# The second layer norm's output, made by VectorE in one pass

## The reference

```python
x = x + _L0_xattn_ref(_layernorm(x), ctx_1024, mask, Wq, bq, Wk, bk, Wv, bv, Wo, bo)
x = x + _L0_ffn_ref(_layernorm(x), theta, phi, theta_noise, phi_noise)

def _layernorm(x, axis=-1, eps=1e-05):
    m = jnp.mean(x, axis=axis, keepdims=True)
    v = jnp.var(x, axis=axis, keepdims=True)
    return (x - m) / jnp.sqrt(v + eps)

# in _L0_ffn_ref
real = jnp.einsum('bti,io->bto', x, jnp.cos(theta + theta_noise))
imag = jnp.einsum('bti,io->bto', x, jnp.sin(phi + phi_noise))
return jnp.sqrt(real * real + imag * imag)
```

## Time and profile before

| | us |
|---|---|
| median of 3 runs | 265.4 (264.9 to 266.73) |
| the profiled execution's own time | 265.45 |
| its span, first to last instruction | 263.6 |
| TensorE busy in the span | 238.0 (90%) |
| VectorE busy | 183.5 (70%) |
| ScalarE busy | 148.7 (56%) |
| GpSimd busy | 65.3 (25%) |

### The profile page before, as it was taken

How to read it: one execution, slowest core, us unless ns; L and a number is a source line. 1 busy time by engine, 2 the same in 40 slices (tenths; PEclk the granted TensorE clock), 3 DMA queues, 4 the chain that set the end, 5 groups by cost and what they waited for, 6 DMA issues and landing times.

```text
span 263.6 us, 3879 instructions
## 1 busy us (share of the span) xinstructions
PE 238.0 (90%) x1223; PEld 135.8 (52%) x1223; DVE 183.5 (70%) x348; ACT 148.7 (56%) x203; POOL 65.3 (25%) x158
## 2 busy tenths in 40 slices
PE   0989859868968799999999999999999999999991
PEld 0979523624633345644664476448545844444440
DVE  2037799996796779678787877787778663964442
ACT  0148667664713792678367647844593559266441
POOL 1000555572524403310331133023302310132000
PEclk9999967999979999999999999999999999999997
DMA  6999930269120797287539635783687244324531
GB/s 201 383 421 413 418 150 0 51 191 236 30 61 18 123 240 298 44 236 180 225 73 245 219 139 122 203 273 106 165 168 316 42 81 80 162 40 80 199 119 44
DMA packets 47948, 44.79 MB, mean 170 GB/s; under 512 B 42454, under 2 KB 42454, under 8 KB 44605
## 3 DMA queue, kind: packets, MB, share of 16 engines
q1 hardware_dynamic: 47269, 44.42, 55.7%
q10 hardware_dynamic: 664, 0.18, 0.4%
HBM read 25.66 MB, written 8.39 MB: 129 GB/s over the span
## 4 chain that ended last, share of the span: by engine, by line
PE 66%; DVE 16%; DMA 5%; POOL 5%; issue 4%; ACT 3%; SPq 1%; DVEq 0%; POOLq 0%; ACTq 0%
PE re L472 7%; PE re L474 7%; PE re L473 7%; PE im L472 7%; PE im L474 7%; PE im L473 7%; PE score_bank L427 6%; DVE angle_w L745 2%; PE att L461 2%; PE att L459 2%; DMA wk<-in_Wk 2%; DVE angle_w L748 2%; DMA xTb<-in_xT 2%; DVE stats L766 2%; DVE x L824 2%
## 5 line engine op out<-in xcount | busy, mean ns | idle before, releaser
L622 ACT ACTIVATE h<-x,shift,rstd 128x512 f32<-128x512 f32 x32 | 25.9, 810 | 40.7 <-POOL shift L348 40.7
L472 PE MATMUL re<-w_hi,hT 128*128 128x512 f16 x108 | 41.6, 385 | 4.2 <-DMA hT<-h_split 4.2
L472 PE MATMUL im<-w_hi,hT 128*128 128x512 f16 x108 | 40.9, 379 | 0.8 <-DVE w_lo L757 0.8
L474 PE MATMUL re<-w_hi,hT 128*128 128x512 f16 x108 | 41.4, 384 | 0.0
L473 PE MATMUL re<-w_lo,hT 128*128 128x512 f16 x108 | 41.4, 384 | 0.0
L474 PE MATMUL im<-w_hi,hT 128*128 128x512 f16 x108 | 40.9, 379 | 0.0
L473 PE MATMUL im<-w_lo,hT 128*128 128x512 f16 x108 | 40.9, 379 | 0.0
L838 DVE SCALAR_TENSOR_TENSOR h_split<-h,h_split 128x512 f16<-128x512 f32 x32 | 22.0, 689 | 20.2 <-ACT h_split L627 20.2
L427 PEld LDWEIGHTS score_bank<-a_keys,xTb 128*128 128x128 f32 x160 | 29.8, 190 | 7.8 <-issue 1.1
L341 POOL TENSOR_TENSOR veps<-mv,eps 128x1 f32<-128x1 f32 x32 | 11.5, 360 | 75.1 <-DVE mv L834 75.1
L633 ACT ACTIVATE sq_re<-re 128x512 f32<-128x512 f32 x32 | 18.6, 586 | 19.3 <-PE re L474 12.7
(11 more groups left out here) (129 smaller groups left out, 392.2 us busy)
## 6 DMA issues: line engine op xcount, KB each, us to landing
xTb<-in_xT SPq DMA_DIRECT2D x8, 1024.0 KB, 5.1
xb<-in_x SPq DMA_DIRECT2D x8, 1024.0 KB, 5.5
out_rows<-wv SPq DMA_DIRECT2D x7, 1024.0 KB, 3.9
wk<-in_Wk SPq DMA_DIRECT2D x2, 512.0 KB, 5.5
wqT<-in_WqT SPq DMA_DIRECT2D x1, 1024.0 KB, 8.5
angle_w<-in_theta SPq DMA_DIRECT2D x2, 512.0 KB, 10.8
angle_n<-in_theta_noise SPq DMA_DIRECT2D x2, 512.0 KB, 11.5
wv<-in_Wv SPq DMA_DIRECT2D x1, 1024.0 KB, 14.0
```

The source lines that it names most:

```text
L472: nc.tensor.matmul(bank_[:, :], hT[j][:, 0, k, :], w_hi[part][:, k, :], start=(k == 0), stop=False)
L474: last = nc.tensor.matmul(bank_[:, :], hT[j][:, 1, k, :], w_hi[part][:, k, :], start=False, stop=(k == CH - 1))
L622: nc.scalar.activation(h[j % 2][:, :], x2[b][:, j, :], ACT.Identity, bias=shift2[:, j:j + 1], scale=rstd2[:, j:j + 1]).then_inc(h_made, 1)
```

## The change

ScalarE's pass that made h, and GpSimd's two operations for the shift, are taken out. VectorE makes h in one instruction, a tensor_scalar that subtracts the mean and multiplies by rstd, both read as one number per partition. ScalarE's `high_half` only makes the f16 high half now. VectorE's order is rewritten around the new step `normal`: `normal(m, j)` stands behind `residual` and statistics of the next tile, and `low_half` of a tile moves back by one place to leave ScalarE time for the high half between them. In a loop step `low_half(n, 2)` and `normal(n, 3)` now stand behind `low_probs`.

```diff
@@ gpsimd, rstd_of_x2 @@
                 nc.gpsimd.tensor_tensor(veps2[:, j:j + 1], mv2[:, j, 1:2], eps[:, 0:1], ALU.add).then_inc(eps2_added, 1)
-                nc.gpsimd.tensor_tensor(minus_mean2[:, j:j + 1], zero[:, :], mv2[:, j, 0:1],
-                                        ALU.subtract).then_inc(minus_mean2_made, 1)
                 pool.wait_ge(eps2_added, TILES * m + j + 1)
                 nc.gpsimd.tensor_tensor(rstd2[:, j:j + 1], veps2[:, j:j + 1], minus_half[:, 0:1], ALU.pow).then_inc(rstd2_made, 1)
-                pool.wait_ge(minus_mean2_made, TILES * m + j + 1)
-                pool.wait_ge(rstd2_made, TILES * m + j + 1)
-                nc.gpsimd.tensor_tensor(shift2[:, j:j + 1], minus_mean2[:, j:j + 1], rstd2[:, j:j + 1],
-                                        ALU.mult).then_inc(shift2_made, 1)
@@ scalar @@
             def high_half(m, b, j):
 
-                if j >= 2 or not isinstance(m, int) or m > 0:
-                    act.wait_ge(lo_made, TILES * m + j - 1)
-                act.wait_ge(shift2_made, TILES * m + j + 1)
-                nc.scalar.activation(h[j % 2][:, :], x2[b][:, j, :], ACT.Identity,
-                                     bias=shift2[:, j:j + 1], scale=rstd2[:, j:j + 1]).then_inc(h_made, 1)
                 act.wait_ge(h_made, TILES * m + j + 1)
@@ vector @@
+            def normal(m, b, j):
+
+                dve.wait_ge(rstd2_made, TILES * m + j + 1)
+                if j >= 2 or not isinstance(m, int) or m > 0:
+                    dve.wait_ge(lo_made, TILES * m + j - 1)
+                nc.vector.tensor_scalar(h[j % 2][:, :], x2[b][:, j, :], mv2[:, j, 0:1], rstd2[:, j:j + 1],
+                                        ALU.subtract, ALU.mult).then_inc(h_made, 1)
+
@@ vector, preparation @@
             mean_of_x2(0, 1)
+            normal(0, 0, 0)
             reduce_angle(1, 0)
             low_half(0, 0)
+            normal(0, 0, 1)
             low_half_of_sine(0, 1)
             residual(0, 0, 2)
             stats_ready(0, 2)
             mean_of_x2(0, 2)
             values_ready(1)
             low_half(0, 1)
+            normal(0, 0, 2)
             reduce_angle(1, 1)
             residual(0, 0, 3)
             stats_ready(0, 3)
             mean_of_x2(0, 3)
             low_half_of_sine(1, 0)
+            normal(0, 0, 3)
@@ vector, block 1 before the loop @@
             mean_of_x2(1, 1)
-            low_half(1, 0)
+            normal(1, 1, 0)
             residual(1, 1, 2)
             stats_ready(1, 2)
             mean_of_x2(1, 2)
-            low_half(1, 1)
+            low_half(1, 0)
+            normal(1, 1, 1)
             residual(1, 1, 3)
             stats_ready(1, 3)
             mean_of_x2(1, 3)
-            low_half(1, 2)
+            low_half(1, 1)
+            normal(1, 1, 2)
@@ vector, loop step @@
                 low_probs(m)
+                low_half(n, 2)
+                normal(n, b, 3)
                 softmax_total(m)
...
                 stats_ready(m, 1)
-                low_half(m, 0)
+                normal(m, a, 0)
                 mean_of_x2(m, 1)
                 residual(m, a, 2)
                 stats_ready(m, 2)
+                low_half(m, 0)
+                normal(m, a, 1)
                 add_squares(n, 2)
                 mean_of_x2(m, 2)
-                low_half(m, 1)
                 residual(m, a, 3)
                 stats_ready(m, 3)
-                low_half(m, 2)
+                low_half(m, 1)
+                normal(m, a, 2)
                 mean_of_x2(m, 3)
```

More of the change, by code:

```diff
@@ L123, in build @@
         eps = sb("eps", [P, TILES])
-        zero = sb("zero", [P, 1])
         xb = [sb(f"xb{i}", [P, TILES, DIM]) for i in range(2)]
@@ L147, in build @@
         rstd2 = sb("rstd2", [P, TILES])
-        minus_mean2 = sb("minus_mean2", [P, TILES])
-        shift2 = sb("shift2", [P, TILES])
         h = [sb(f"h{i}", [P, DIM]) for i in range(2)]
@@ L205, in build @@
         stats2_made, mean2_made, eps2_added, rstd2_made = (sem(f"{n}") for n in ("stats2_made", "mean2_made", "eps2_added", "rstd2_made"))
-        minus_mean2_made, shift2_made = sem("minus_mean2_made"), sem("shift2_made")
         h_made, hi_made, lo_made = sem("h_made"), sem("hi_made"), sem("lo_made")
@@ L315, in _ @@
             nc.gpsimd.memset(eps[:, :], LN_EPS)
-            nc.gpsimd.memset(zero[:, :], 0.0)
             nc.gpsimd.memset(p_split[:, :, STACK:2 * P], 0.0).then_inc(pad_made, 1)
@@ L988, in _ @@
             step(6, 0, None)
+            low_half(LAST, 2)
+            normal(LAST, 1, 3)
             add_squares(LAST - 1, 3)
```

## The result

The changed kernel takes 270.6 us (median of 4 runs, 270.28 to 272.54) against 265.4 of the kernel before: 1.020 times the time, 95% interval 1.016 to 1.025. Its profiled execution took 270.28 us, with a span of 268.5 us, 4.9 more than before.

What follows compares the result with a forecast made beforehand. The kernel's end was taken to be set by when TensorE gets through its first 102 us. Block 1 4.7 us late, less a vanished 0.65 us hole, gave 265.45 + 4.05 = 269.5 us, range 266.1 to 272.3.

Steps and rivals of the forecast that it cites:

- the likeliest case: Slower through VectorE's longer preparation and block 1's later start, with a low-clock stretch behind both holes: 269.5 us, chance 0.50.
- What the change adds: One VectorE pass per tile, 0.43 us with the clamp as model, or 0.69 without the doubled rate.
- step 1: VectorE's preparation to 60 us: four passes (1.4 us) and two waits for GpSimd (1.65) delay the imaginary feeds 3.1 us.
- Step 2: TensorE from 63.1 us: a hole of about 5 us, then a 1.7 us low-clock loss; attend(1,1,1) 1.0 us late.
- step 3: Block 1 waits 2.0 us more for its first hT, starting 3.0 late; a second low stretch makes it 4.7.
- Step 4: The loop costs nothing, but keeps margins of only 0.3, 1.2 and 1.3 us.
- The second rival: Passes take 0.69 us, or the loop's thin margins break, or both: 271 to 272.8 us, chance 0.20.
- The first rival: The clock does not fall at one of the two holes, or at neither: 266.1 to 267.8 us, chance 0.23.
- The third: Rival, not slower: GpSimd has each deviation ready, VectorE's chain grows by 1.4 us alone: 264.4 us, chance 0.07.

Runs made afterwards that it cites:

- e1: The changed kernel with block 0's four tiles of h made as before (ScalarE's pass, GpSimd's shift, VectorE's old order): 268.31 us, ratio 1.009.
- e4: The changed kernel with 16 + 3 idle matmuls in TensorE's hole before the imaginary feeds and 17 before block 1: 267.29 us, ratio 1.0055.
- e2: The changed kernel with only the first three tiles of block 1 made as before, low halves in their old places: 268.82 us, ratio 1.010.
- e6: The changed kernel with normal(1,0) ahead of residual(1,1) and low_half(1,0) between that residual and its statistics: 268.69 us, ratio 1.013.
- e3: The changed kernel with block 0 and the first three tiles of block 1 made as before, the loop as changed: 266.64 us, ratio 1.0036.
- e7: The changed kernel with the load of transposed x ahead of the transpose of h's fourth tile on SyncE's queue: 271.40 us, ratio 1.020.
- e11: The changed kernel with both holes filled by idle matmuls and the load of transposed x first: 266.08 us, ratio 1.0033.
- e8: The changed kernel with later passes in block 0, early pass and low half for block 1's tile 0, transposed x first, both holes filled: 263.76 us, ratio 0.995.
- e9: The changed kernel with block 0 as before, early pass and low half for block 1's tile 0, transposed x first, 9 idle matmuls before attend(1,1,0): 264.35 us.
- e10: The mixed kernel (block 0 by ScalarE, the rest by VectorE, its other edits kept) with 9 more idle matmuls before block 1: 263.72 us, ratio 0.994.
- e12: The kernel before, without the new pass, with transposed x loaded first and 9 idle matmuls each before attend(1,1,0) and block 1: 263.98 us, ratio 0.995.
- e5: The changed kernel with normal(0,2) and normal(0,3) moved back past an instruction or more, for GpSimd's deviation to be ready: 269.98 us, ratio 1.015.

## Why the prediction was right

**The forecast** was 269.5 us in a range of 266.1 to 272.3; measured were 270.6. The direction, the stage and the mechanism were those of the likeliest case.

**What the change adds, the pass.** Predicted 0.43 us, measured 0.541. A tensor_tensor of the same 128x512 f32, the sum of squares, took 0.683. With 0.51 us for 512 columns at the plain rate the new pass would have a fixed part of 0.03, where the prediction's rows gave 0.17; at the doubled rate it has 0.28. That speaks for the doubled rate and a fixed part about 0.1 us larger than the clamp's with its constants; one size alone can't separate the two. The Trainium skill's page "VectorE: DVE Perf Modes" (section "The perf-mode tier table"), which gives f32 tensor_scalar in SBUF twice tensor_tensor's rate, agrees with this. The clamp as the model was 0.1 short, 0.4 us over the four passes of step 1.

**Step 1, VectorE's chain.** Predicted 3.1 us later. From the sum of the probabilities (39.62, before 39.42) to the end of the last low half of a sine, VectorE needs 3.4 us more: four passes of 0.46 back to back, and 1.4 of waits. The two waits for GpSimd are there, 0.71 each instead of 0.85 and 0.8, at 52.95 and 60.04. The add took 1.14 and 1.08 us, beside VectorE's low halves (h's at 51.56, the sine's at 58.13), which read two tensors in SBUF. The Trainium skill ("GPSIMD Engine Reference", section "Key points") names instructions with two SBUF inputs among those that contend with GpSimd, and the two rows agree. e1 takes the step away, and the distance from the first feed to the imaginary ones is again 9.44 us, as before.

**Step 2, first low stretch.** Predicted 78.9 for attend(1,1,0) and 81.9 for attend(1,1,1), measured 79.22 and 82.25, 1.35 late instead of 1.0. The hole and the low stretch at 76.2 are gone and one behind 63.6 has come. e4 shows its price together with that of step 3's: 3.3 us for both, predicted 3.4.

**Step 3, block 1.** Predicted 8.2 us from attend(1,1,1) to block 1, measured 8.26; a hole of 4.1, measured 4.20; 1.7 us for the low stretch behind it, and the place 97.45 (attend(2,0,0) before) moved to 102.57, 5.1 late where I had 4.7. e2 and e6 change the order ahead of that low half and both move block 1's start.

**Step 4, the loop, is the term that was off.** I put it at nothing with a margin of 0.3 us for the load of transposed x, and that margin was read from one loop step (issue at 171.38, first use at 178.01: 6.63 us). The second step was tighter even before. There, in the kernel before:

```profile
122.07 0.43 SPq L225 DMA_DIRECT2D xTb<-in_xT  x1
...
127.37 0.34 PE L427 MATMUL score_bank<-a_keys,xTb 128*128 128x77 f32 x2
```

and in the changed kernel:

```profile
126.97 0.43 SPq L221 DMA_DIRECT2D xTb<-in_xT  x1
...
131.90 0.45 PE L416 MATMUL score_bank<-a_keys,xTb 128*128 128x77 f32 x2 [0.17 <-DMA xTb<-in_xT]
```

From issue to first use were 5.30 us. In the changed kernel the use would come at 131.56, 4.59 after the issue, and a load needs about 5. In the third to fifth step 5.01 to 5.24 us are left, just enough or short by 0.05. The steps with a load took 4.45, 4.89, 4.50, 4.49 and 4.45 us from attend(m, 1) to attend(m, 2), 0.5 us too much. By it one loop step took 25.76 us, over the 25.4 that the prediction named as a sign of being wrong. TensorE's weight loads show whom they wait for (us in total, times, longest):

```profile
PEld score_bank L416 <- DMA xTb<-in_xT: 1.1, 3, 0.7
```

e3 has the same wait with all else ahead of the loop as before, e7 and e11 take it away. The second rival named it; it cost 0.5 us here and 0.7 in e3, not the 1.5 I had as its price.

**The sum.** 3.4 late at block 1, 1.7 for the low clock, 0.9 back from the wait for transposed x in the first step (I had 0.65), 0.5 in the loop: 4.7 at the last attention matmul (238.77 against 234.05), 4.9 in the span, 4.8 in the profiled time. I had 4.05. Of the 0.7 too little, 0.4 stem from the passes and step 1 and 0.5 from the loop, less 0.3 for the first step's wait.

**The first rival**, a clock that stays up, did not happen in the profiled execution. The length of a low stretch does vary, though: 3.5 us in the changed kernel behind the first hole, 5.0 in e6 and 5.2 in e2 with the same hole, 5.2 in e7 behind the second. That 1.7 us was right for both here is in part luck. **The third**, not slower, fell with GpSimd's slow add.

**Open** is why my sums for e8, e9, e10 and e12 were each 1 to 1.7 us too low. In e9 it is the low stretch that I had not counted, in e10 a part is the wait for the probabilities. e12's profiled execution took 262.59 us, the fastest of its twelve, and 0.7 us of that is an early start: its first feed is at 49.90 where the other traces with block 0 as before have 50.6. Its trace shows no hole that would explain the other eleven, of which there are no traces.

## What to carry to other kernels

A pass moved from an idle engine to a fuller one is judged where the fuller engine is the chain: here the loop had 6 us of VectorE to spare and hid 1.8 us a step but for some late loads, while four passes in the preparation and one pass with a residual ahead of the first low half cost about 4 us. A margin in a loop is to be read in every step: the one that broke was the tightest of those that had held before. A per-partition scalar made by a third engine must be ready when its reader comes, and a small instruction on GpSimd took six times its length beside a busy VectorE. Look at TensorE's holes before counting microseconds of delay: here a hole of 4 us cost its length and then half the time of the low clock behind it. Filling the holes with idle matmuls gave back 3.3 us at once, where no re-ordering alone gave over 2; with the holes filled the re-orderings gave another 2.3. And give the old kernel the same remedies before the new one is judged: it became faster by them, too.

## What the runs showed of the hardware

- A tensor_scalar of 128x512 f32 in SBUF with two per-partition scalars took 0.52 to 0.55 us, where a tensor_tensor of that size took 0.683 and a tensor_scalar with two constants 0.693 for 1024 columns.
- TensorE's clock fell to its lower level behind holes of 1.81 (e1), 2.12 (before), 2.21 (e9), 2.45 (e2) and about 4.2 us, and stayed up behind others of 1.77 (e6), 2.12 (before) and 2.91 us (e3). The same gap ahead of the imaginary feeds was followed by the low clock in e3 and not in the kernel before, so the length of a hole alone did not decide. The low stretches lasted 3.4 to 5.2 us. With both holes filled by matmuls (e4) the clock stayed at 1.00.
- On GpSimd, an add on 128x1 f32 in the changed kernel took 0.19 us in the loop, and 1.14 and 1.08 us at two places of the preparation, beside VectorE instructions without a gap; in e5 one took 2.28, and the power 2.01 instead of 0.55.
- The load of 1 MB of transposed x took 5.0 us from issue to landing (the median in the changed kernel). A step that left 4.59 us for it waited 0.4 us, steps that left 5.01 and 5.04 lost 0.05, one that left 5.24 nothing.
